# Two gates in one accumulator, and new engine queues, in a four-layer graph kernel on one Trainium2 core

## What is computed

```python
h = x
for _ in range(3):
    a_in = einsum('nm,bmd->bnd', adj, h); a_out = a_in
    av = concatenate([a_in, a_out])
    z = sigmoid(av @ w3.T + w3_b + h @ u3.T + u3_b)          # update gate
    r = sigmoid(av @ w4.T + w4_b + h @ u3.T + u3_b)          # reset gate
    hv = tanh(av @ w5.T + w5_b + (r * h) @ u5.T + u5_b)      # candidate
    h = (1 - z) * h + z * hv
```

## Time and profile before

| | |
|---|---|
| median of 3 runs | 1342.25 us (1340.95 to 1342.89) |
| profiled execution | span 1341.3 us, mean granted TensorE clock 0.996 |
| busy: TensorE, weight load | 96%, 84% |
| busy: VectorE, ScalarE, GpSimd | 80%, 53%, 40% |
| DMA | 29.19 MB, mean 22 GB/s |

### The profile page before, as it was taken

One profiled execution on the slowest core, in us unless ns is written; L12 is line 12 of the kernel. 1 busy time (PEld: TensorE's weight loads), 2 busy tenths in 40 slices (PEclk: granted clock), 3 DMA queues, 4 the chain that ended last, 5 costly groups with the idle time before them and its releaser, 6 DMA issues.

```text
span 1341.3 us, 21962 instructions
## 1 busy us (share of the span) xinstructions
PE 1283.5 (96%) x7912; PEld 1130.6 (84%) x7912; DVE 1074.2 (80%) x2110; ACT 714.1 (53%) x1229; POOL 530.3 (40%) x586
## 2 busy tenths in 40 slices
PE   7899999999999999999999999999999999999995
PEld 6788898888979889898888988889898888988795
DVE  5579788797878968788797887978789687885897
ACT  5655555545555555555555655455555555556541
POOL 1135343443443434443353444443534343441254
PEclk9999999999999999999999999999999999999998
DMA  5010100001000010000001001010000100000000
GB/s 173 1 32 1 40 10 16 31 0 47 0 20 27 0 47 0 31 16 16 31 0 47 0 16 31 0 47 0 31 16 0 47 0 31 16 16 1 1 1 32
DMA packets 29386, 29.19 MB, mean 22 GB/s; under 512 B 2352, under 2 KB 28464, under 8 KB 29360
## 3 DMA queue, kind: packets, MB, share of 16 engines
q1 hardware_dynamic: 27808, 28.32, 6.4%
q0 software_dynamic: 192, 0.52, 0.2%
q10 hardware_dynamic: 1360, 0.01, 0.1%
HBM read 20.45 MB, written 8.39 MB: 22 GB/s over the span
## 4 chain that ended last, share of the span: by engine, by line
PE 75%; DVE 14%; issue 5%; POOL 4%; DMA 1%; ACT 1%; DVEq 0%; ACTq 0%; POOLq 0%
PE b_ps L482 35%; PE f_ps L482 35%; DVE b_a_lo L1352 3%; POOL b_rstd L366 2%; PE f_ps L579 2%; DVE normed L1324 2%; DVE hb_feat L1285 2%; DVE b_a_lo L1259 1%; POOL b_var_eps L364 1%; PE b_ps L579 1%; PE b_ps L596 1%; DMA bias_in<-in_L_gnn_u_b 1%; DVE f_cand L1279 1%; PE b_ps L627 1%; DVE hb_node_lo L1299 1%
## 5 line engine op out<-in xcount | busy, mean ns | idle before, releaser
L364 POOL TENSOR_TENSOR b_var_eps<-b_moments,eps 128x2 f32<-128x2 f32 x120 | 34.6, 288 | 339.4 <-DVE b_moments L1313 339.3
L350 POOL TENSOR_TENSOR f_kept<-f_kept,hf_feat 128x512 f32<-128x512 f32 x66 | 91.0, 1379 | 169.7 <-ACT f_kept L941 169.6
L1324 DVE TENSOR_SCALAR normed<-summed,b_moments,b_rstd 128x256 f32<-128x256 f32 x180 | 96.5, 577 | 6.5 <-POOL b_rstd L366 6.5
L375 POOL TENSOR_TENSOR skip<-normed,bias_out 128x512 f32<-128x512 f32 x60 | 88.1, 1469 | 10.3 <-DVE normed L1324 10.3
L366 POOL TENSOR_TENSOR b_rstd<-b_var_eps,neg_half 128x2 f32<-128x2 f32 x120 | 86.1, 718 | 9.4
L350 POOL TENSOR_TENSOR b_kept<-b_kept,hb_feat 128x512 f32<-128x512 f32 x30 | 45.7, 1525 | 110.5 <-ACT b_kept L941 110.5
L1306 DVE BATCH_NORM_STATS2 b_stats<-summed 128x6 f32<-128x256 f32 x240 | 88.4, 410 | 0.8 <-issue 0.3
L946 ACT ACTIVATE f_cand<-f_ps,bias_c 128x512 f32<-128x512 f32 x66 | 45.5, 690 | 63.8 <-PE f_ps L482 63.5
L890 ACT ACTIVATE f_a_hi<-f_ps 128x512 fp32r<-128x512 f32 x68 | 40.6, 598 | 71.6 <-PE f_ps L482 69.9
L890 ACT ACTIVATE b_rh_hi<-b_ps 128x512 fp32r<-128x512 f32 x90 | 53.6, 596 | 45.4 <-PE b_ps L482 45.4
L482 PE MATMUL f_ps<-adjT_hi,hf_node_hi 128*128 128x256 f32 x264 | 75.8, 287 | 0.3 <-POOL hf_node_lo L338 0.3
(11 more groups left out here) (330 smaller groups left out, 5081.6 us busy)
## 6 DMA issues: line engine op xcount, KB each, us to landing
x_front<-in_x SPq DMA_DIRECT2D x16, 512.0 KB, 3.5
x_back<-in_x SPq DMA_DIRECT2D x15, 512.0 KB, 3.5
out<-result SPq DMA_DIRECT2D x15, 512.0 KB, 3.0
x_back<-in_L_gnn_u_w SPq DMA_DIRECT2D x2, 256.0 KB, 9.2
bias_out<-in_L_gnn_bias POOLq DMA_DIRECT2D x4, 128.0 KB, 6.7
b_z<-in_L_gnn_w_w SPq DMA_DIRECT2D x1, 512.0 KB, 11.6
b_gate<-in_L_gnn_w_w SPq DMA_DIRECT2D x1, 512.0 KB, 12.5
b_kept<-in_L_gnn_w_w SPq DMA_DIRECT2D x1, 512.0 KB, 13.0
```

Source lines behind the costliest of these rows:

```text
L350: pool.tensor_tensor(L.kept[:, k], L.kept[:, k], L.state.feat[:, k], ALU.mult).then_inc(L.s_kept, 1)
L364: pool.tensor_tensor(Y.var_eps[:, g], Y.moments[:, g, :, 1], eps[:], ALU.add).then_inc(Y.s_var, 1)
L375: pool.tensor_tensor(Y.skip[:, g], Y.normed[:, g], bias_out[:, j], ALU.add).then_inc(Y.s_skip, 1)
L1324: last = dve.tensor_scalar(dst[:, g, c], Y.summed[:, g, c], Y.moments[:, g, c, 0:1], Y.rstd[:, g, c:c + 1], ALU.subtract, ALU.mult)
```

## The change

Both gates now build up in the same bank of `ps0`. `base` writes h u3; `reset` adds a w4 on top (`start=False`); `reset_gate` takes the sigmoid from `ps0` with the reset bias; then `update` adds a (w3 - w4) on top, so that `ps0` holds a w3 + h u3. The difference of the weights is made once, before the loop (`update_minus_reset`), and `w34T` takes the place of `w3T`. `keep_base` and `reset_arg` are gone, with their semaphores. `update` waits for `reset_gate` of its half; `candidate_mixed` waits for `a_lo` alone. The lists of all four engines in `body` and `finish` are ordered anew.

```diff
             def reset(L, n, k):
                 pe.wait_ge(L.s_a_lo, upto(n))
-                product(L.ps1[:, k], columns(w4T, k), mixed(L)).then_inc(L.s_reset, 1)
+                product(L.ps0[:, k], columns(w4T, k), mixed(L), start=False).then_inc(L.s_reset, 1)
             def update(L, n, k):
-                pe.wait_ge(L.s_a_lo, upto(n))
-                pe.wait_ge(L.s_base_kept, upto(n, k))
-                product(L.ps0[:, k], columns(w3T, k), mixed(L), start=False).then_inc(L.s_update, 1)
+                pe.wait_ge(L.s_r, upto(n, k))
+                product(L.ps0[:, k], columns(w34T, k), mixed(L), start=False).then_inc(L.s_update, 1)
             def candidate_mixed(L, n, k):
-                pe.wait_ge(L.s_reset_arg, upto(n, k))
+                pe.wait_ge(L.s_a_lo, upto(n))
                 product(L.ps1[:, k], columns(w5T, k), mixed(L), stop=False)
...
-            def keep_base(L, n, k):
-                act.wait_ge(L.s_base, upto(n, k))
-                act.activation(L.gate[:, k], L.ps0[:, k], ACT.Identity, bias=bias_r[:, k:k + 1]).then_inc(L.s_base_kept, 1)
             def reset_gate(L, n, k):
-                act.wait_ge(L.s_reset_arg, upto(n, k))
-                act.activation(L.gate[:, k], L.gate[:, k], ACT.Sigmoid).then_inc(L.s_r, 1)
+                act.wait_ge(L.s_reset, upto(n, k))
+                act.activation(L.gate[:, k], L.ps0[:, k], ACT.Sigmoid, bias=bias_r[:, k:k + 1]).then_inc(L.s_r, 1)
...
+            def update_minus_reset():
+                dve.wait_ge(s_halves, 2)
+                dve.tensor_tensor(w3_nat[:, :, 0:D], w3_nat[:, :, 0:D], w4_nat[:, :, 0:D],
+                                  ALU.subtract).then_inc(s_halves, 1)
-            def reset_arg(L, n, k):
-                dve.wait_ge(L.s_base_kept, upto(n, k))
-                dve.wait_ge(L.s_reset, upto(n, k))
-                dve.tensor_tensor(L.gate[:, k], L.ps1[:, k], L.gate[:, k], ALU.add).then_inc(L.s_reset_arg, 1)
...
             sum_halves(w3_nat, "w3")
+            update_minus_reset()
             prep_lo(2, prep_bank(2))
             for k in range(C):
                 a_lo(front, 0, k)
             sum_halves(w5_nat, "w5")
```

In the old lists VectorE had, at the second convolution, `normalise(2,0); candidate_part 0; normalise(2,1); conv_x_lo(1,0); hand_over_h 0; conv_x_lo(1,1)`, and TensorE had `base 0; turn_h3 0; base 1; turn_h3 1` and `candidate_mixed 0; turn_x1 0; candidate_mixed 1; turn_x1 1; candidate_reset 0`. In `finish`, among much else:

```diff
                 turn_input(LAST, 0)
-                mix(back, LAST - 1, 0)
+                for k in range(2):
+                    mix(back, LAST - 1, k)
+                base(back, LAST - 1, 0)
                 turn_input(LAST, 1)
-                base(back, LAST - 1, 0)
-                mix(back, LAST - 1, 1)
+                base(back, LAST - 1, 1)
...
                 mix_nodes(last_pair, 0, 0, 0)
+                convolve(last_pair, 0, 0, 0)
                 mix_nodes(main, LAST - 1, 0, 0)
-                convolve(last_pair, 0, 0, 0)
                 convolve(main, LAST - 1, 0, 0)
```

More of the change, by code:

```diff
@@ L764, in finish @@
                 for k in range(2):
+                    mix(front, 2 * LAST + 1, k)
+                for k in range(2):
+                    base(front, 2 * LAST + 1, k)
+                for k in range(2):
+                    reset(front, 2 * LAST + 1, k)
+                candidate_mixed(front, 2 * LAST + 1, 1)
+                for k in range(2):
+                    update(front, 2 * LAST + 1, k)
+                candidate_mixed(front, 2 * LAST + 1, 0)
+                for k in range(2):
+                    candidate_reset(front, 2 * LAST + 1, k)
@@ L765, in finish @@
+                candidate_reset(back, LAST - 1, 0)
+                update(back, LAST - 1, 1)
+                for k in range(2):
                     turn_h(state_f, 2 * LAST + 2, k)
-                for k in range(2):
-                    candidate_reset(back, LAST - 1, k)
+                candidate_reset(back, LAST - 1, 1)
                 for k in range(2):
                     mix(front, 2 * LAST + 2, k)
-                base(front, 2 * LAST + 2, 0)
                 for k in range(2):
-                    turn_h3(main, LAST - 1, k)
@@ L1004, in body @@
                 rh_hi(back, q, 0)
+                input_nodes_hi(p, 1)
+                rh_hi(back, q, 1)
                 keep_gate(back, q, 0)
[L1006 to L1016 removed]
@@ L1030, in body @@
-                feat_hi(state_f, 2 * p + 1, 0)
-                candidate(front, 2 * p, 1)
+                input_hi(p, 1)
+                update_gate(back, q, 0)
+                candidate(back, q, 0)
+                keep_gate(back, q, 1)
+                a_hi(front, 2 * p, 0)
+                update_gate(back, q, 1)
+                candidate(back, q, 1)
+                a_hi(front, 2 * p, 1)
+                for k in range(2):
+                    reset_gate(front, 2 * p, k)
+                rh_hi(front, 2 * p, 0)
@@ L1100, in finish @@
-                keep_base(front, 2 * LAST + 1, 0)
-                reset_gate(back, LAST - 1, 1)
+                    reset_gate(front, 2 * LAST + 1, k)
+                rh_hi(back, LAST - 1, 1)
+                for k in range(2):
+                    rh_hi(front, 2 * LAST + 1, k)
                 keep_gate(back, LAST - 1, 0)
                 for k in range(2):
-                    a_hi(front, 2 * LAST + 1, k)
-                rh_hi(back, LAST - 1, 0)
-                update_gate(back, LAST - 1, 1)
@@ L1191, in _ @@
             act.wait_ge(s_bias, 4)
-            for k in range(C):
-                keep_base(front, 0, k)
             for i in (3, 4, 5):
@@ L1210, in _ @@
                 prep_hi(i)
-            for k in range(C):
-                keep_base(front, 1, k)
             for k in range(C):
@@ L1385, in body @@
                 for k in range(2):
-                    reset_arg(back, q, k)
-                for k in range(2):
                     reset_h(back, q, k)
@@ L1668, in _ @@
                 prep_lo(i, prep_bank(i))
-            for k in range(C):
-                reset_arg(front, 0, k)
             for k in range(C):
@@ L1697, in _ @@
                 a_lo(front, 1, k)
-            for k in range(C):
-                reset_arg(front, 1, k)
             for k in range(C):
```

593 lines of the change are left out of this document (272 added, 321 removed).

## The result

The changed kernel takes 1350.15 us (median of 4 runs, 1346.56 to 1350.74) where the kernel before, on the same chip, takes 1341.71 (4 runs, 1340.95 to 1342.89). The ratio is 1.0055, with a 95% interval of 1.0042 to 1.0067: slower. The forecast was 1328.4. Beside the experiments further down the kernel before was timed again, with medians of 1341.5 to 1342.9. Of the ten executions of gates_only one took 2364 us at a granted clock of 0.84, a slower state that is not compared. The profiled execution spans 1348.0 us against 1341.3, and the mean granted clock of TensorE is 0.981 against 0.996.

A forecast was written before the change was run, and what follows sets the result against it. TensorE, busy 96% of the span, was taken as the bound. Loop -11.9, `finish` -2.5 and before the loop +0.6 made -13.8 us, from 1342.25 to 1328.4 us; range 1308 to 1345.

The forecast's parts named there:

- the second convolution's: In each body, GpSimd blocks two VectorE operations, so TensorE waits 1.75 us plus 0.1 before `mix_nodes(1,1)`.
- the slower rival: At the second convolution three blocks, waits of 3.85 us per body, +0.8 us per body, 1351 us; chance 0.18.
- The waits: In each loop body, TensorE waits 2.2 us in all against 2.8 before: -0.6 us per body.
- the back step: In each body up to the attention, everything is covered, some places tightly; 0.1 us of wait allowed.
- the attention: In each body, `attend(1)` needs `values_lo(1)`, either 0 or 0.5 us late; taken as 0.25 us.
- The work taken away: Per body ScalarE -3.8 us and VectorE -4.1 us, by themselves worth 0 because TensorE waits for neither's throughput.
- finish: After the loop, reordering removes waits for `feat_lo` (-0.8) and `hf_feat` (-1.5); with fewer switches -2.5 us in all.
- Before the loop: `update_minus_reset` is one more VectorE operation ahead of `sum_halves(w5)`, which TensorE waits for: +0.6 us.
- the switches: In each body, switches from transposes to products fall from 9 to 6, at 0.08 us each: -0.25 us.
- the likeliest case: Two blocks at the second convolution: 1328.4 us, own range 1320 to 1336; chance 0.5.
- port is free: At the second convolution one block or none is left: 1313 us, or 1297 with no wait at all; chance 0.2.

The follow-up runs named there:

- gates_only: Kernel before with both gates in `ps0`, old lists kept but for what must drop, `reset_gate(front, 2p, 1)` ahead of `update_gate(front, 2p, 0)`: 1342.1 us.
- one_wait: Kernel before with one line added: TensorE waits for both `conv_x_lo` ahead of the first `mix_nodes(1,0)`, joining two waits: 1399.18 us.
- keep_late: pool_late with GpSimd's `keep(front, 2p+1, 1)` also held back until `conv_x_lo(1,1)` is done: 1303.81 us.
- fill24: Changed kernel with 24 unused matmuls between `mix_nodes(1,0)` and `mix_nodes(1,1)` in each body: 1339.53 us.
- fill12: Changed kernel with 12 unused matmuls between `mix_nodes(1,0)` and `mix_nodes(1,1)` in each body: 1331.08 us.
- fill4: Changed kernel with 4 unused matmuls between `mix_nodes(1,0)` and `mix_nodes(1,1)` in each body: 1331.36 us.
- pool_late: Changed kernel with GpSimd's two `add_bias` of the second convolution held back until `hand_over_h(1)` is done: 1309.93 us.

## Why the prediction was wrong

**The step that failed** is the second convolution's: "two 1.75 ... plus 0.1 for the restart", with which the body's waits became "2.2 us against 2.8: -0.6 per body". A wait was priced at its length plus 0.1, whatever its length. In the kernel before that held, for waits of 0.41, 1.31 and 0.77. But the change gathers the last two into one of 2.09, and behind it the clock falls. The rows to see it were in hand: the prediction quotes the slow starts behind the 2.5 us wait of `finish`, "about 1.6 lost", and does not ask what they mean for a wait of 1.85 us in a loop, between the 1.31 that did no harm and the 2.5 that did. Twelve times 1.5 is 18 us. No rival had this mechanism; the slower rival (three blocks, 1351) has the measured time almost to the microsecond, and for another reason: its waits of 3.85 us per body are not there.

**What held.**
- *The waits.* Forecast 1.85 at `mix_nodes(1,1)` and 2.2 in all; measured 2.09 + 0.11 = 2.20. That the sums agree to the hundredth is luck. The allowances of 0.1 for the back step and 0.25 for the attention were not used up by anything; the port took some 0.35 more than two blocks of 1.1, since it caught both halves of `normalise` (2.07), as the slower rival had said it could, and half of `conv_x_lo` (0.51). `reset(back)`, `mix_nodes(1,0)`, `update`: no wait, as forecast.
- *The work taken away* is worth 0: gates_only, with VectorE 4.1 us and ScalarE 3.6 us emptier per body, for a forecast of 4.1 and 3.8. With the new order VectorE is 8.4 us emptier (66.55 to 58.14): the other half is blocking, which the prediction's figure of 4 us did not count.
- *finish*: -3.7 for -2.5. The waits for `hf_feat` (1.4), `hb_feat_lo` (0.7) and GpSimd's `f_sq_lo` (1.6) are gone, and new ones for `f_rh_lo` and `b_rh_lo` have come.
- *Before the loop*: +0.3 for +0.6. This says little: with the same instructions in it, this part took 58.15 us in the kernel before and 56.41 in one_wait.

**A term mis-sized: the switches,** -0.25 a body. The old body without its waits is 78.4 us; the new one is too (keep_late: 78.57 less its 0.16; fill24: 81.2 less 24 matmuls of 0.1175): the term is 0 or hardly more. Each switch saved is paid back in the transposes. Of the kernel before (4 transposes ahead of the matmul in the earlier trace rows), then of the kernel after (8):

```profile
568.35 0.60 PE L579 MATMUL b_ps<-ident,b_cand 128*128 128x128 f32 x4
```

```profile
574.06 1.04 PE L576 MATMUL b_ps<-ident,b_cand 128*128 128x128 f32 x8
574.85 0.48 PE L480 MATMUL f_ps<-f_a_hi,w4T_hi 128*128 128x512 f32 x1
575.17 0.39 PE L480 MATMUL f_ps<-f_a_lo,w4T_hi 128*128 128x512 f32 x1
```

Four take 568.70 - 568.35 = 0.35 and the switch 0.09: twice that is 0.88. Eight take 0.79 and the switch 0.09: 0.88. The saving that the 0.32 seemed to promise was counted from one side of the group alone.

**The sum again,** with these sizes: waits 14 × (-0.6) = -8.4, switches 0, clock +18 (12 bodies, 1.5 each), the first body +0.7 (it is 1.0 us longer than the others, 0.3 in the kernel before), `finish` -3.7, before the loop +0.3: +6.9 on the span, for a measured 6.7. With the clock's term alone missing it would be about 1342 - 11 = 1331, inside the likeliest case's own range of 1320 to 1336, and fill12 and fill4 measured 1331.

**The rival "port is free"** gave 1313 for one block left and 1297 for none. It didn't come about by itself, but pool_late (one block: 1309.9) and keep_late (none: 1303.8) are these kernels. What the second lies above its 1297 is mostly the switches (14 × 0.25 = 3.5), the wait of 0.16 (2.2) and the first body, 1 us longer than the rest.

**A reading that was off.** The prediction puts `normalise` among the operations "with both inputs in SBUF". Its row has one input of that size in SBUF, `summed`, and it was blocked all the same. The Trainium skill ("SBUF — State Buffer", "Who interferes with whom") says that a VectorE operation with at most one input in SBUF does not contend outside a special mode, and names `tensor_scalar`, which `normalise` is, among those that can enter that mode. The rows agree with this: `normalise` was blocked, and `sum_conv` with its operand in PSUM kept its 0.68.

The Trainium skill says in the same section that the order of issue decides who blocks. By recorded starts the rows agree only in part. In keep_late `candidate_part` started 0.18 us ahead of `keep` and kept its 0.69, while `keep` took 1.67. But in the kernel after `normalise(2,1)` started at 621.39, 0.06 us ahead of `keep`, and it was `normalise` whose first half took 1.49 instead of some 0.4, with `keep` at its 1.29, in all 14 bodies. The second half then stood behind GpSimd's next operation. Why a recorded lead of 0.06 us did not protect the first half stays open.

**Left open.** The beat on which the falls stand is read from the trace and was not tested. The Trainium skill ("TensorE: Matmul & The Clock Gate", Part 1) says that the number of slow matmuls varies between executions of the same kernel; here the fall itself comes or not between passes of the same loop, 2 of 14 without it, and between two kernels with the same wait of 2.70 us.

## What to carry to other kernels

Price a wait of TensorE together with the clock behind it: when an edit joins several short waits into one, look at every wait of about that length, in more than one trace, and at how far apart the starts behind it are, since one that kept the clock may have been lucky in its place; a few unused matmuls in the middle of it are the quick test. Where GpSimd and VectorE share a port, look for GpSimd's operations with time to spare and hold them behind the VectorE chain that TensorE waits for; then look at once at what the held-back operation meets next. A saving on one side of a group of instructions is only one when the whole group, from the start before it to the start behind it, has become shorter.

## What the runs showed of the hardware beyond what was expected

- Adding matmuls made the kernel faster: 56 of them (fill4), by 19 us.
- Behind the loop's wait the clock never fell at 1.62 us (fill4, 14 bodies), fell at 2.09 us in 12 of 14 bodies, 0.06 to 1.17 us after the restart, and at 3.67 us in all 14 (one_wait), in 13 of them already before the restart; a fall cost 1.5 us at 2.09 and some 2.6 at 3.67.
- The length of the wait is not all: of two equal waits of 2.70 us in `finish` one lost the clock (before) and one kept it (gates_only), and the falls of the kernel after begin 81.92 us apart or twice that, in bodies of 82.1.
- GpSimd's operations back to back and VectorE's interleave, one against one: the two halves of a `normalise`, 0.73 us of work together, took 1.49 and 1.39 us.
